# Unread products on TensorE in the transformer node stage of a four-layer graph network

## What is computed

```python
x = _layernorm(x + _L0_gnn_ref(x, src, dst, ...))          # gated differences
x = _layernorm(x + _L1_gnn_ref(x, src, dst, edge_weight, ...))  # attention, 4 heads
x = _layernorm(x + _L2_gnn_ref(x, edge_index, edge_attr_32, ...))  # transformer, 8 heads
x = _layernorm(x + _L3_gnn_ref(x, edge_index, ...))        # two GAT layers
```

```python
out = agg.reshape(n, H) @ Wo + bo
x = _layer_norm(x + out, ln1_g, ln1_b)
h = gelu(x @ W1 + b1) @ W2 + b2          # 128 -> 512 -> 128
return _layer_norm(x + h, ln2_g, ln2_b)
```

## Time and profile before

| | us |
|---|---|
| median of 3 runs (6671.12 to 6688.41) | 6677.1 |
| profiled execution, span | 7599.6 |
| PE busy | 1283.1 (17%) |
| DVE busy | 4666.3 (61%) |
| ACT busy | 1410.9 (19%) |
| POOL busy | 4386.9 (58%) |
| node stage of the transformer, from its first gather to the last table row | 4853 to 5157 |
| start of the x1 turn in rounds 0 to 6 | 4878.5, 4914.0, 4946.6, 4988.1, 5029.3, 5062.4, 5096.8 |

### The profile page before, as it was taken

The page is one execution under the profiler, slowest core; times in us unless marked ns, Lnnn a source line. Parts: engine busy times, 40 slices in busy tenths (PEclk is TensorE's granted clock), DMA queues, the critical chain, the costliest instruction groups (busy, mean ns, idle before and its releaser), DMA issues. The chain is left out here.

```text
span 7599.6 us, 37104 instructions
## 1 busy us (share of the span) xinstructions
PE 1283.1 (17%) x8049; PEld 1112.1 (15%) x8049; DVE 4666.3 (61%) x9328; ACT 1410.9 (19%) x3648; POOL 4386.9 (58%) x4445
## 2 busy tenths in 40 slices
PE   7100000143443333333000000370000001000000
PEld 6100000033343333332000000250000001000000
DVE  7677777687676667996677777544443434433435
ACT  0122212220000002442000000262222211222223
POOL 1666566545565554005666666426777767777775
PEclk9555555555555555556555555585555555555555
DMA  9555445323333224773555555203333332333332
GB/s 347 179 181 185 164 161 171 120 85 103 101 109 103 95 98 157 296 268 91 176 179 174 180 179 181 85 20 93 106 99 101 101 90 66 111 102 101 97 100 80
DMA packets 338944, 1032.97 MB, mean 136 GB/s; under 512 B 100325, under 2 KB 163137, under 8 KB 331294
## 3 DMA queue, kind: packets, MB, share of 16 engines
q0 software_dynamic: 166752, 401.68, 18.9%
q1 hardware_dynamic: 116642, 342.34, 12.9%
q10 hardware_dynamic: 55324, 286.57, 10.1%
HBM read 602.97 MB, written 427.39 MB: 136 GB/s over the span
## 5 line engine op out<-in xcount | busy, mean ns | idle before, releaser
L708 POOL DMA_INDIRECT rows<-table,idx x3136 | 3091.7, 986 | 1446.0 <-issue 1022.3
L635 POOL DMA_INDIRECT by_src<-ebuf,place x784 | 767.8, 979 | 561.4 <-DVE place L1277 295.9
L1280 DVE SCALAR_TENSOR_TENSOR psA<-psA,cont,dstf 128x128 f32<-128x128 f32 (+1 forms) x2349 | 838.0, 357 | 291.2 <-remote 205.9
L1269 DVE TENSOR_TENSOR sc<-rows,ebuf 128x56 f32<-128x56 f32 x112 | 28.2, 252 | 1196.5 <-DMA rows<-table,idx 1196.5
L1280 DVE SCALAR_TENSOR_TENSOR sums<-sums,cont,psA 128x128 f32<-128x128 f32 (+1 forms) x1512 | 521.2, 345 | 225.0 <-remote 139.9
L934 PE MATMUL psA<-dstf,ones 128*128 128x512 f32 x10 | 9.9, 1113 | 3446.9 <-DVE dstf L2169 3446.9
L803 PE MATMUL psA<-attr,sums 128*128 128x49 f32 x1568 | 406.0, 403 | 747.4 <-DVE attr L1458 735.3
L803 PEld LDWEIGHTS psA<-attr,sums 128*128 128x128 f32 x1568 | 397.0, 326 | 761.1 <-DVE attr L1458 748.7
L934 PEld LDWEIGHTS psA<-dstf,ones 128*128 128x128 f32 x10 | 2.7, 318 | 3448.6 <-issue 3448.6
L2050 DVE TENSOR_TENSOR_SCAN psA<-rows,psA 128x1980 f32<-128x1980 f32 x112 | 480.0, 4286 | 3.9
L1211 ACT ACTIVATE psA<-df 128x60 f32<-128x60 f32 (+1 forms) x168 | 40.4, 241 | 2104.9 <-DVE df L1269 1120.4
(11 more groups left out here) (332 smaller groups left out, 5548.4 us busy)
## 6 DMA issues: line engine op xcount, KB each, us to landing
dstf<-spread_wide SPq DMA_DIRECT2D x168, 924.0 KB
states<-sums ACTq DMA_DIRECT2D x150, 952.0 KB, 3.7
rows<-by_src SPq DMA_DIRECT2D x55, 1035.0 KB, 5.1
states<-sums ACTq DMA_DIRECT2D x56, 1008.0 KB
spread_wide<-sums SPq DMA_DIRECT2D x56, 924.0 KB, 24.3
states<-sums ACTq DMA_DIRECT2D x56, 903.0 KB
rows<-table,idx POOLq DMA_INDIRECT x3136
msg<-low_rows SPq DMA_DIRECT2D x56, 448.0 KB
```

The lines of the kernel that those rows point to most:

```text
L635: pool.indirect_dma_start(by_src[:, :], bass.IndirectOffsetOnAxis(ap=place[:, s, j:j + 1], axis=0), payload[:, s, j, :], None).then_inc(so ...
L708: pool.indirect_dma_start(rows[:, at:at + GW[ph]], None, table[ph][:, :], bass.IndirectOffsetOnAxis(ap=idx[:, s, j:j + 1], axis=0)).then_i ...
L1269: return dve.tensor_tensor(o_, a_, b_, op)
L1280: return dve.scalar_tensor_tensor(o_, a_, s_, b_, op0, op1)
```

## The change

In stage `ph == 3` TensorE gets a helper that runs bf16 products of `onesb` and `bias3f` (256 columns) into the first 256 columns of `psT`. Nobody reads them; the next turn overwrites them. It is called with 12 at the start of every turn (ahead of the wait for its input), with 48 before and 24 after `project(0)`, and with 20 ahead of the fifth of the eight feed-forward products in rounds 1 to 6, before that product's wait for its GELU. They signal nothing and wait for nothing. The start value of `holds` is another from stage 3 on.

```diff
--- before.py
+++ after.py
@@ -811,8 +811,14 @@
             xt = Steps(n_xT)
             gel = Steps(n_gelu)
             for ph in range(5):
+                def keep_warm(times):
+
+                    for _ in range(times):
+                        pe.matmul(psT[:, 0:2 * D], onesb[:, :], bias3f[:, :], start=True, stop=True)
+
                 def turn_x(tile, ready, count):
 
+                    keep_warm(12)
                     pe.wait_ge(ready, count)
                     turn(KB, lambda b: tile[:, b, 0:D]).then_inc(n_t, 1)
                     xt.add()
@@ -843,12 +849,16 @@
 
                 if ph == 3:
                     pe.wait_ge(bias3f_ready, 1)
+                    keep_warm(48)
                     project(0)
+                    keep_warm(24)
                     for k in range(KG):
                         turn_x(x1s[k % 2], x1_ready, k + 1)
                         for i in range(8):
                             if i >= 2:
                                 gel.add()
+                                if k and i == 4:
+                                    keep_warm(20)
                                 pe.wait_ge(n_gelu, gel.value())
                             pe.matmul(psM[:, 2 + i % 2, 0:448], W1[:, i // 2 * P:(i // 2 + 1) * P],
                                       xT[:, i % 2 * 448:(i % 2 + 1) * 448], start=True, stop=True).then_inc(n_ff, 1)
@@ -2007,7 +2017,7 @@
                 su = Steps(sums_ready, NG * ph)
                 ru = Steps(rows_used, 2 + NG * TURN.get(ph, 0))
                 sr = Steps(scores_ready, NG * ph)
-                holds = Steps(hold_step, (B - 1) * NG * ph)
+                holds = Steps(hold_step, (B - 1) * NG * min(ph, 2))
                 accs = Steps(acc_step, (B - 1) * NG * ph)
                 parts = Steps(msg_ready)
                 wide = int(ZW[ph] == ROW)
```

## The result

| | before | changed |
|---|---|---|
| median, us | 6677.2 (20 runs, 6667.4 to 6688.4) | 6691.7 (20 runs, 6685.8 to 6695.4) |
| ratio | | 1.0021 (95% interval 1.0014 to 1.0027) |
| profiled execution, span | 7599.6 | 6687.9 |
| median forecast | | 6694 (6672 to 6716) |

The change costs 14.5 us, 0.2%: slower, and inside what counts as the same.

A forecast was written before the change was run, and what follows sets the result against it. Gathers and VectorE's edge passes bound the kernel, but the node stage's TensorE-ScalarE relay adds directly to it. Costs 23.6 + 3.7 less 5, 2.4 and 2 give +17.9, taken as +17: 6694 us, range 6672 to 6716.

The forecast's parts named there:

- The price of a product, 0.11 and 0.213 us: Time of each added TensorE product, at full and half clock, taken from an earlier stage's bias products of the same shape.
- 18 groups lie on the chain with their whole length, 23.6 us: Three turns in each of rounds 1 to 6: every group of 12 delays the chain fully, 23.6 us at full clock.
- The 48, the 20 and the last 12 are hidden: Before project(0), mid feed-forward and before the last table turn: added products fall into waits and cost nothing.
- Six groups after products 6 and 7 are partly at half clock, 0.6 us more each: Groups of 12 behind the last two feed-forward products: half of each at half clock, adding 3.7 us.
- The clock falls in nearly every round still: Before the last two feed-forward products the gap stays near 4 us, so 14 us of possible gain don't come.
- Round 0 gives 5 us back: The 36 products before round 0 raise the clock for its turn, feed-forward and Wo: 60% of 8 us.
- One more spell, 2 us back: Another half-clock stretch, 5095 to 5104.5 us of the profile: up to 4 us to regain, half counted.
- The sum: Whole stage: 23.6 + 3.7 - 5 - 2.4 - 2 = +17.9 us, taken as +17.
- The 922 us between span and median: Profiled execution 7599.6 us against median 6677.1 without profiler; stage's turns and products assumed equally long in both.
- The clock holds: Rival: full clock through the whole stage, net -2 us, 6675 us; chance 16%.
- The added products fall into stalls: Rival: added products in TensorE stalls beside gathers cost 0.6 us more each, 6708 to 6727 us; 17% together with all-half-clock.

The follow-up runs named there:

- e2: Changed kernel with only the 12 products ahead of each turn kept, without the 48, 24 and 20: 6694.5 us, 1.0021 of before.
- e7: Changed kernel with 44 instead of 20 products in the middle of the feed-forward: 6676.0 us, 1.0004 of before.
- e6: Changed kernel without the 12 per turn and the 48, with 36 after the first projection and 44 mid feed-forward: 6650.5 us, 0.9967 of before.
- e4: Changed kernel with 24 instead of 12 products ahead of each turn: 6709.0 us, 1.0053 of before.
- e3: Changed kernel with only the 48 and 24 products around the first projection kept: 6675.5 us, 0.9995 of before.
- e10: Kernel before plus 12 products ahead of the table rows' turn alone: 7574.0 us, 1.0009 of before, in a comparison where before took 7574 us.
- e1: Changed kernel without the 12 products ahead of each turn, keeping the 48, 24 and 20: 6680.9 us, 0.9999 of before.
- e8: Kernel with 36 and 44 products, plus 128 ahead of the stage's last turn: 7581.5 us, 1.0009 of before, where before took 7574 us.
- e9: Kernel before plus only 32 products in the middle of the feed-forward: 7563.1 us, 0.9983 of before, where before took 7574 us.
- e5: Changed kernel with only the products in the middle of the feed-forward, 44 instead of 20: 6652.0 us, 0.9966 of before.
- e11: Kernel with 36, 44 and 128 products (the last ahead of the stage's last turn), measured again: 6650.3 us, 0.9961 of before.

## Why the prediction was right, and where not

The cost side was right in mechanism and size; what the clock gives back was mis-sized in two terms, and that the number came within 3 us is in part luck.

- **The price of a product, 0.11 and 0.213 us:** right, 0.109 at full clock in groups of 12 and 24; at half clock the 12 of e2 take 2.72 us, (2.72 - 0.42)/11 = 0.209 with the tail of the earlier trace rows.
- **18 groups lie on the chain with their whole length, 23.6 us:** right (e7 against e6, 3.89 us for the three groups of a round and 25.5 us in the medians; e4). The count is right, but one of the 18 stands in round 0, ahead of the turn of round 1's head, and round 6 has two.
- **The 48, the 20 and the last 12 are hidden:** right. More than that: 44 are hidden in the middle. The work that covers them is ScalarE's normalisation.
- **Six groups after products 6 and 7 are partly at half clock, 0.6 us more each:** they are five, since round 6 has no such turn. They take 1.47, 2.14, 2.29, 2.35 and 2.39 us, 3.3 us more in all, where 3.7 were forecast.
- **The clock falls in nearly every round still:** right, in each of the six, though in e4 it held twice over the same gap.
- **Round 0 gives 5 us back:** mis-sized. The 36 end 2.9 us before the turn, and it runs at half clock. Round 0 is even 1.2 us longer than in the second profile of before, because two groups of 12 lie on its chain (2.6 us): 1.4 us back. The 8 us came from a round of 35.6 us that had stalls in it; undisturbed it takes 23.6 and gets full clock within its eight products by itself. e3 shows what is to be had, 2.1 us.
- **One more spell, 2 us back:** mis-sized the other way. The first profile of before had one second spell, the second profile has three at some 3.8 us each, and the profile of the changed kernel has none. From the x1 turn of round 1 to that of round 6 the changed kernel takes 184.9 us instead of 174.9: 15 groups x 1.3 = 19.6 and the 3.3 at half clock, so 12.9 back. Two such spells are 7.6 and the turn behind products 6 and 7 at full clock (0.93 instead of 1.65 us) 3.6. What is left, 1.7 us, goes with rounds 1 and 2, where the clock was at 1.00 again from 4204.5 and from 4242.1 us on, before or during the 12 products; they take 36.2 and 36.4 us, the other three 37.4 and 37.5.
- **The sum.** The costs were forecast at 27.3 us and are 26.9 (23.6 + 3.3). The clock was to give back 9.4; between the two profiles, whose stages differ by 9.5 us, it gave back 17.4, and by the medians, which differ by 14.5, it gave back 12.4. How many second spells an execution has differs, the prediction had nothing that says how many, and e2 and e10 show that the 12s don't rule them out. So the closeness of 14.5 to 17 rests partly on luck.
- **Why executions differ.** The granted clock that is listed for each whole execution speaks for the spells: of the 27 runs of before beside e1 to e3 the three fastest have 0.533 to 0.534 and the three slowest 0.532 (correlation of time and clock -0.78), of e1's eleven the fastest has 0.535 and the slowest 0.532 (-0.88). In the 17 runs of before beside e4 to e7 it is only -0.38, so the spread of 21 us has other parts too.
- **The 922 us between span and median:** not the profiler's load. The profiled executions of before and after with spans of 6680.3 and 6687.9 us agree with the medians.
- **The rivals.** "The clock holds": its sum (6675 us, 16%) is what e7 measured, 6676.0, but it takes 44 products in the middle and not 20. "The added products fall into stalls": none stood in the trace of the changed kernel, and where stalls came (e8 to e10) no added product was slowed.

## What to carry to other kernels

Products that only keep TensorE busy are free where the engine would wait in any case, and cost their full length where it comes straight from work with its input ready: put them by the wait, not by the kind of step. Size them to the gap: 20 of them that left 3.9 us gained nothing, 44 that left 1.25 us gained 0.34%. Where the gap was 5.81 us the clock was lost every time (before, e2, e3), at 3.86 us in 16 rounds of 18 (the changed kernel, e1, e4), at 2.55 us in 3 of 6 (e9), and at 1.25 us in none of 24 (e5, e6, e7, e11). And look at more than one round and more than one execution of the kernel before, since the same loop can run with one half-clock spell a round or with two.

## What was not expected of the hardware

A loop with a fixed body has rounds of two lengths, according to whether the clock falls a second time at the table products. In e1 (20 in the middle, no 12s) this came five times, in the second profile of before three times, in e3 once; whether the 20 products bring it about is not shown, since the median of e1 is that of before. It does not need the first spell: in e11 it came in a round in which the clock had held over products 6 and 7. In the profiles of e5 and e6, with the gap cut from 5.81 to 1.25 us, both kinds of spell are gone, and a round is 1.7 to 6.5 us shorter than in the second profile of before. And the same kernel took 6680 us in one comparison and 7574 us in another on the same chip, with W2 products that followed each other at 0.7 to 2.1 us beside the gathers; what that is, no run settled.
